# A transformer block on one core: transposes moved ahead of gate and up products, mask rows in fp32r, null products opened in one piece

## What is computed

```
xn  = ln(x, g_norm)
q   = l2norm((xn @ Wq) per head) * q_scale          # 16 heads of 64
k,v = xn @ Wkv (one head for all), one null key and value in front
sim = q @ k.T * 8 + bias[head, i - j], masked (causal, and by row)
x   = x + ln(softmax(sim) @ v @ Wout, g_out)
scores = softmax((x @ wt.T + g @ wg.T) / 2), best 2 of 8 experts, weights normed
y   = sum over experts of w_e * (leaky(x @ w_gate) * (x @ w_up)) @ w_down
y  += (leaky(x @ sw_gate) * (x @ sw_up)) @ sw_down  # shared, 2 blocks of 128
x   = x + y
```

## Time and profile before

| | |
|---|---|
| time, median of 3 runs | 1070.17 us (1069.21 to 1070.3) |
| the profiled execution, its time | 1068.73 us |
| its span, first to last instruction | 1066.9 us |
| TensorE busy | 1011.4 us (95%) |
| VectorE busy | 725.8 us (68%) |
| ScalarE busy | 541.0 us (51%) |
| GpSimd busy | 438.6 us (41%) |
| granted TensorE clock, mean | 0.998 |

### The profile page before, as it was taken

One profiled execution on the slowest core, in us unless ns is written; L12 is line 12 of the kernel. 1 busy time (PEld: TensorE's weight loads), 2 busy tenths in 40 slices (PEclk: granted clock), 3 DMA queues, 4 the chain that ended last, 5 costly groups with the idle time before them and its releaser, 6 DMA issues.

```text
span 1066.9 us, 22567 instructions
## 1 busy us (share of the span) xinstructions
PE 1011.4 (95%) x7300; PEld 823.6 (77%) x7300; DVE 725.8 (68%) x2497; ACT 541.0 (51%) x1596; POOL 438.6 (41%) x422
## 2 busy tenths in 40 slices
PE   3877999999999999999999999999999999999998
PEld 2765877878787887878777787787878788787877
DVE  8889487665867558665677647766586755866543
ACT  3598256652565435663456515665256643566220
POOL 1644254441454333642535515444145433354212
PEclk9999999999999999999999999999999999999999
DMA  5326423111132013311132212311113210221043
GB/s 198 73 77 209 138 69 121 51 60 62 61 110 89 36 47 100 100 61 61 42 114 77 69 42 72 119 49 62 62 61 110 89 37 29 96 103 62 36 133 105
DMA packets 41004, 87.79 MB, mean 82 GB/s; under 512 B 4193, under 2 KB 19041, under 8 KB 40625
## 3 DMA queue, kind: packets, MB, share of 16 engines
q1 hardware_dynamic: 39920, 83.57, 23.9%
q10 hardware_dynamic: 960, 2.62, 0.7%
HBM read 76.57 MB, written 9.60 MB: 81 GB/s over the span
## 4 chain that ended last, share of the span: by engine, by line
PE 70%; DVE 15%; issue 6%; ACT 3%; DVEq 0%; POOL 0%; ACTq 0%; POOLq 0%
PE psY L1647 13%; PE psS L1517 6%; PE psO L1553 5%; PE psG L71 5%; PE psG L69 5%; PE psG L70 5%; PE psT L1528 5%; PE psS L1512 3%; PE psS L69 2%; PE psS L71 2%; PE psS L70 2%; PE psT L1535 2%; PE psO L1556 2%; DVE work L423 2%; PE psT L69 2%
## 5 line engine op out<-in xcount | busy, mean ns | idle before, releaser
L592 POOL TENSOR_TENSOR work<-work,rden 128x514 f32<-128x514 f32 x128 | 134.2, 1049 | 328.6 <-DVE rden L1143 328.1
L1647 PE MATMUL psY<-Wd,H 128*128 128x256 f32 x640 | 171.7, 397 | 0.0
L757 ACT ACTIVATE work<-work,low 128x257 f32<-128x257 f32 x256 | 128.5, 504 | 63.5 <-DVE low L1161 63.5
L69 PE MATMUL psG<-x1T_hi,Wgu 128*128 128x512 f32 (+1 forms) x292 | 134.6, 461 | 3.5 <-ACT leaky L801 1.9
L1647 PEld LDWEIGHTS psY<-Wd,H 128*128 128x128 f32 x640 | 111.6, 189 | 28.1 <-issue 14.4
L1161 DVE CUSTOM_DVE_ANT_0 work<-psS,bias,null_s 128x256 f32<-128x256 f32 x256 | 113.1, 478 | 22.3 <-PE psS L1517 19.4
L1257 DVE SCALAR_TENSOR_TENSOR leaky<-leaky 128x512 f32<-128x512 f32 x80 | 55.4, 692 | 93.3 <-ACT leaky L801 93.3
L71 PE MATMUL psG<-x1T_lo,Wgu 128*128 128x512 f32 (+1 forms) x292 | 114.7, 393 | 0.0
L70 PE MATMUL psG<-x1T_hi,Wgu 128*128 128x512 f32 (+1 forms) x292 | 113.7, 389 | 0.0
L581 POOL TENSOR_TENSOR rq<-qss,neghalf 128x16 f32<-128x16 f32 x32 | 97.5, 3049 | 34.4 <-DVE qss L1137 34.4
L761 ACT ACTIVATE work<-work,low 128x129 f32<-128x129 f32 x256 | 99.4, 390 | 0.0
(11 more groups left out here) (264 smaller groups left out, 2567.6 us busy)
## 6 DMA issues: line engine op xcount, KB each, us to landing
Wgu<-wexp SPq DMA_DIRECT2D x80, 512.0 KB, 3.4
Wb<-wscr SPq DMA_DIRECT2D x64, 256.0 KB, 3.6
wexp<-Wgu SPq DMA_DIRECT2D x10, 512.0 KB, 2.9
xres<-in_x SPq DMA_DIRECT2D x8, 512.0 KB, 4.0
xin<-in_x SPq DMA_DIRECT2D x7, 512.0 KB, 4.1
out<-work SPq DMA_DIRECT2D x7, 512.0 KB, 3.2
H<-in_wgu SPq DMA_DIRECT2D x10, 256.0 KB, 3.5
bias<-bscr SPq DMA_DIRECT2D x4, 512.0 KB, 6.2
```

Of the source, the lines that this page charges most:

```text
L69: te.matmul(dst, a_hi, b_hi, start=start, stop=False)
L592: pool.tensor_tensor(T1[sl][:, hs, :], T1[sl][:, hs, :], rden[sl][:, 1, hs].unsqueeze(2) .to_broadcast([P, 2, N + 1]), ALU.mult)
L757: act.activation(T1[sl][:, h, :], T1[sl][:, h, :], ACT.Exp, scale=-1.0, bias=low[sl][:, 1, h:h + 1], accum_out=den[sl][:, 1, h:h + 1])
L1647: mm = te.matmul(psY[:, t // 2, (t % 2) * D:(t % 2 + 1) * D], H[:, k % H_RING, t * P:(t + 1) * P], Wd[:, ORDER[k], :], start=(k == 0 and t ...
```

## The change

Three things are edited. First, on TensorE `turn` now stands ahead of `gate` and `up` in a step, on VectorE `leak` and `hidden` stand behind `turned`, and on ScalarE `take_gate` behind `turned`. Second, `pick_bf` and `MK` become fp32r (`pick` is built in a buffer that `leaky` uses later, and copied). Third, the four null products stand in front of the output projection's products, the first two ahead of the waits for `o_done` and `h_done`, and open the banks instead of closing them.

```diff
-        pick_bf = sb("pick_bf", [P, P], BF16)
+        pick = sb("pick", [P, P], F32R)
...
-        MK = sb("MK", [P, BB, N + P], BF16)
+        MK = sb("MK", [P, BB, N + P], F32R)
...
                     if n < ALL:
                         exps(r, n // STEPS, n % STEPS)
-                    if moe is not None and n in GATE_AT:
-                        take_gate(moe, GATE_AT[n])
...
                     if TURN_LAG <= n < ALL + TURN_LAG:
                         turned(r, n - TURN_LAG)
+                    if moe is not None and n in GATE_AT:
+                        take_gate(moe, GATE_AT[n])
...
+            pre(dve.tensor_copy(pick[:], leaky[0][:, 0:P]))
...
-                    if moe is not None and n in GATE_AT:
-                        leak(moe, GATE_AT[n])
-                    if moe is not None and n in UP_AT:
-                        hidden(moe, UP_AT[n])
...
                         turned(r, n - TURN_LAG)
                         if (n - TURN_LAG) % STEPS == STEPS - 1:
                             null_turned(r, (n - TURN_LAG) // STEPS)
+                    if moe is not None and n in GATE_AT:
+                        leak(moe, GATE_AT[n])
+                    if moe is not None and n in UP_AT:
+                        hidden(moe, UP_AT[n])
...
+                    if n == TURN_LAG:
+
+                        need(te, qT_a, r, 2 * TILES)
+                        need(te, qT_v, r, 2 * TILES)
+                    if TURN_LAG <= n < ALL + TURN_LAG:
+                        turn(r, n - TURN_LAG)
+                    if moe is not None:
                         if n in GATE_AT:
                             gate(moe, GATE_AT[n])
                         if n in UP_AT:
                             up(moe, UP_AT[n])
-                    if n == TURN_LAG:
-
-                        need(te, qT_a, r, 2 * TILES)
-                        need(te, qT_v, r, 2 * TILES)
-                    if TURN_LAG <= n < ALL + TURN_LAG:
-                        turn(r, n - TURN_LAG)
...
-                need(te, o_done, r, ALL)
                 need(te, s1_read, r, ALL)
                 need(te, s0_read, r, ALL)
                 for t in range(TILES):
+                    if t == 2:
+                        need(te, o_done, r, ALL)
+                        if moe is not None:
+
+                            need(te, h_done, moe, BLOCKS)
+                    te.matmul(wo_banks[t], PNT[:, t * P:(t + 1) * P], Unull[:], start=True, stop=False)
+                for t in range(TILES):
                     if t == 2 and following is not None:
                         keys(following)
-                    if t == 2 and moe is not None:
-
-                        need(te, h_done, moe, BLOCKS)
                     dst = wo_banks[t]
                     for p in range(PAIRS):
-                        products(te, dst, [part[:, p, t * P:(t + 1) * P] for part in qT],
-                                 [part[:, p, :] for part in Wout], p == 0, False)
-                    te.matmul(dst, PNT[:, t * P:(t + 1) * P], Unull[:], start=False, stop=True) \
-                        .then_inc(wo_ps.sem, 1)
+                        mm = products(te, dst, [part[:, p, t * P:(t + 1) * P] for part in qT],
+                                      [part[:, p, :] for part in Wout], False, p == PAIRS - 1)
+                    mm.then_inc(wo_ps.sem, 1)
...
-                    te.matmul(psS[:, i, 0:N + P], pick_bf[half, :], MK[half, bb, :], start=True, stop=False)
+                    te.matmul(psS[:, i, 0:N + P], pick[half, :], MK[half, bb, :], start=True, stop=False)
```

More of the change, by code:

```diff
@@ L11 @@
 F32 = mybir.dt.float32
-BF16 = mybir.dt.bfloat16
 F32R = mybir.dt.float32r
@@ L830, in pre @@
                 return count[0]
-            for ap, v in ((leaky[0][:], 0.0), (mask8[:], 0), (pick_bf[:], 0.0), (pick_bf[0:1, :], 1.0), (pick_bf[DH:DH + 1, :], 1.0),
+            for ap, v in ((leaky[0][:], 0.0), (mask8[:], 0), (leaky[0][0:1, 0:P], 1.0), (leaky[0][DH:DH + 1, 0:P], 1.0),
                           (PNT[:], 0.0), (Unull[:], 0.0),
@@ L1458, in attention @@
                             down(moe, *DOWN_AT[LAST_DOWN])
[L1459 to L1462, removed]
                     if n == TURN_LAG:
@@ L1468, in attention @@
                         turn(r, n - TURN_LAG)
+                    if moe is not None:
+                        if n in GATE_AT:
+                            gate(moe, GATE_AT[n])
+                        if n in UP_AT:
+                            up(moe, UP_AT[n])
                 need(te, pn_done, r, GROUPS)
```

## The result

The changed kernel takes 1076.23 us (median of 6 runs, 1075.02 to 1077.6), the kernel before, run beside it, 1069.07 us: a ratio of 1.0067, with an interval of [1.0054, 1.008]. It is slower by 7.2 us. One of six executions of the last kernel under the experiments took 1160.14 us at a granted clock of 0.825 and is in no median here. The profiled execution took 1077.21 us, its span 1075.4 us (1066.9 before).

A forecast was written before the change was run, and what follows sets the result against it. TensorE bounds seven of eight rounds (98% busy). Fp32r mask rows 10.3 and round 0 0.5, less 1.4 for the wait, give +9.4 us: 1078.1 profiled, 1079.6 as median; own range 1075.8 to 1083.6, 8-in-10 range 1070 to 1084.

The forecast's parts named there:

- Seams of format cost nothing: On TensorE, between fp32 and fp32r products of the same array shape: a change of format costs 0 us.
- Seams of shape cost the drain and the first load: On TensorE, where array shape changes: 0.09 to 0.10 us drain, plus a shown load of 0.014 to 0.104.
- Part 2: Mask rows in fp32r: 0.09 us load plus 0.015 stream per pair, 98 pairs in rounds 1 to 7, 10.3 us.
- 0.5 for round 0: Fp32r mask rows in round 0: a third of 16 pairs paid, 0.5 us (0 to 1.7).
- Part 1: New order in a step: the 0.23 us wait at step 13 goes in six rounds, -1.4 us.
- Part 3: Null products moved to the front of the output projection: 0 us, bounds 0 and +0.5.
- A: Mask rows behind gate or up: same format removes drain and load, -7.4 us, 1062.8 us; chance 0.10.
- B: Mask rows: the fp32r load shows no more than the bf16 one, about +0.2, 1070.3 us; chance 0.06.
- C: Mask rows: the two halves' loads come one after the other, another 10.5 us, 1090; chance 0.03.
- D: Gate steps: leaky behind the transposes holds back VectorE until mask rows wait, +15 us, 1094; chance 0.02.

The follow-up runs named there:

- the last kernel under the experiments: New order and null products with bf16 mask rows, transposes also ahead of the down products, against the kernel before: 1063.77 us, ratio 0.995.
- the doubled pair: Kernel before with fp32r mask rows issued twice in a step: 1095.28 us in a single execution, 16.6 over the profiled one with them once.

## Why the prediction was right, and where its sizes were off

The forecast was the likeliest case, +9.4 us; measured are +7.2. It came true by its mechanism, and two small terms were mis-sized, both as too small a gain. The time measured, 1076.2, stands only 0.4 us above the lower end of my own range, 1075.8.

- **Seams of format cost nothing:** right. Putting fp32r mask rows behind an fp32r gate took nothing away (0.33 us, of which 0.10 is the delay of the change of shape), and the order on all three engines gave no more, as far as the runs tell apart, than the order of VectorE and ScalarE alone (-1.8 and -1.4 us in the traces).
- **Seams of shape cost the drain and the first load:** right, and the load is shown from three sides. Its 0.10 follows the product that stands first (score pair first, mask in bf16: the same price), is paid once (the doubled pair), and is less for transposes (0.05) than for down products (0.10); why, when both have weights of 128 fp32 columns, no run tells. The delay ahead of it (0.09 to 0.10) is the same for bf16 and fp32r openers; that it is a drain is my reading, and no run tests it.
- **Part 2, 0.105 us a step in 14 steps of seven rounds:** right. Steps 2 to 14 grew by 0.10 to 0.12 (step 12 too, once the gain of its wait is taken off), steps 0 and 1 not at all. The 0.5 for round 0 can't be told from its scatter, and `MK` in fp32r cost VectorE nothing (552 ns both ways; I had allowed up to 1.0 us). The mask rows alone, by the same terms without the gain at step 13 and without the surplus that its wait hides in six rounds, give 92 x 0.105 + 0.5 = 10.2; measured +10.5.
- **Part 1, -1.4 us:** the right wait, the right cause, the wrong size. I took the 0.23 us listed as the gain. Between starts it was 0.31, so 1.8 or 1.9 in six rounds (order alone: 1.8 in the trace, 2.2 by the medians).
- **Part 3, null products at 0:** this is the term that failed. I weighed the end of the projection (which tile is done when) and h_done, and never asked whether the first product waits. It waited for `o_done`, 0.2 us a round with the product behind it, and null products in front fill that time. Alone they are worth -1.2 us in the trace and -1.4 by the medians; on top of the order 0.6 and 0.2, with a part given back at `turn_x1`.
- **The rest:** the price of fp32r in rounds 1 to 6 (8.3 measured, 8.8 by 84 x 0.105), less 1.9 for the wait and less 0.6 to 1.2 for the null products, gives 5.2 to 6.3; the trace has 5.9. And the kernel before ran at 1069.1 here instead of the 1070.2 from which I counted, which is a third of the 3.4 us between 1079.6 and 1076.2.
- **Rivals:** A (the seam becomes free) is refuted by the gate-to-mask seam, B (the fp32r load shows no more than bf16) by 0.40 against 0.30, C (two loads in series) by a price of 0.10 and not 0.2, D (VectorE holds up mask rows) by the list of waits, where mask rows have none that is new (the wait at `turn_x1` stands outside the steps and comes with the null products).

## What to carry to other kernels

When a block of products begins with another array shape, put the product with the shortest weight load first there. In this kernel a bf16 one of 64 rows by 128 columns showed 0.014 us, while fp32 and fp32r ones showed 0.05 to 0.10 each time they stood at the seam, and nothing behind it. Don't convert such an opener for uniformity; formats side by side were free. And before you price a reordering at nothing, look at both ends of the block for a wait of the first instruction, and measure it from start to start, since the idle time listed (0.23) fell short of what its removal gave (0.31).

## What the runs showed that I had not expected

VectorE's leaky step, whose operands didn't change, is listed with a mean of 692 ns before and 750 after. By source line (least, median, largest ns), before and then after:

```profile
L1257 DVE SCALAR_TENSOR_TENSOR leaky<-leaky x80: 677/692/942, 144.5 to 1057.7; 128x512 f32<-128x512 f32 x80
```

```profile
L1257 DVE SCALAR_TENSOR_TENSOR leaky<-leaky x80: 674/691/1548, 145.7 to 1066.2; 128x512 f32<-128x512 f32 x80
```

The median stands still and a few become long: 8 of 80 are over 0.8 us after, one for each expert part, and 1 before. With the order of VectorE and ScalarE alone it is 8 too, with the mask rows alone 2. One such took 1.23 us while GpSimd was in a product of its own (both engines' timeline, after):

```profile
564.03 1.29 POOL L605 TENSOR_TENSOR H<-H,Wb 128x512 f32<-128x512 f32 x1
564.63 1.23 DVE L1257 SCALAR_TENSOR_TENSOR leaky<-leaky 128x512 f32<-128x512 f32 x1 [1.83 <-ACT leaky L800]
```

All 8 run beside a product of GpSimd's line 605, and none of the 37 leaky steps with no product of GpSimd beside them took over 0.70 us; but 8 others that met line 605 stayed short. So the new order makes the two meet, and what they contend for was not tested. TensorE's waits for `leaky` and `H` stay as they were (1.9 and 1.7 us over the run, 1.9 and 1.6 before).
